# One vector through one partition and TensorE, and GpSimd's two kinds of values made together, in a four-layer graph attention kernel

## The reference

```python
h = jnp.einsum('nf,hfd->hnd', x, W)                 # 4 heads of 64
s_src = jnp.einsum('hnd,hd->hn', h, a[:, :64, 0])
s_dst = jnp.einsum('hnd,hd->hn', h, a[:, 64:, 0])
e = jax.nn.leaky_relu(s_src[:, :, None] + s_dst[:, None, :], 0.01)
e = jnp.where(adj[None, :, :] == 0, -jnp.inf, e)
out = jnp.einsum('hij,hjd->hid', jax.nn.softmax(e, axis=-1), h)
```

## Time and profile before

| | |
|---|---|
| median of 3 runs | 2998.18 us (2996.25 to 3000.05) |
| the profiled execution | 2995.74 us |
| its span, first to last instruction | 2993.9 us |
| TensorE busy | 2923.0 us, 98% |
| VectorE, ScalarE, GpSimd busy | 2133.9, 1920.6, 1179.6 us |
| mean granted clock of TensorE | 0.994 |

### The profile page before, as it was taken

How to read it: one execution, slowest core, us unless ns; L and a number is a source line. 1 busy time by engine, 2 the same in 40 slices (tenths; PEclk the granted TensorE clock), 3 DMA queues, 4 the chain that set the end, 5 groups by cost and what they waited for, 6 DMA issues and landing times.

```text
span 2993.9 us, 65253 instructions
## 1 busy us (share of the span) xinstructions
PE 2923.0 (98%) x24628; PEld 2556.9 (85%) x24628; DVE 2133.9 (71%) x3887; ACT 1920.6 (64%) x3414; POOL 1179.6 (39%) x1559
## 2 busy tenths in 40 slices
PE   7999999999989999999999999999999999989999
PEld 6899999999979999999998878887788878755555
DVE  5999898888888888888896556566666656562245
ACT  4777999999988999999985545444455444430000
POOL 0672385641226565654121023333323333444222
PEclk9999999999999999999999999999999999999999
DMA  8677100000100000000010000000000000000001
GB/s 292 207 234 246 39 11 15 11 11 14 62 15 13 11 15 11 15 11 15 11 35 12 4 1 4 4 1 4 1 4 4 1 1 1 3 1 1 0 14 42
DMA packets 41912, 104.55 MB, mean 35 GB/s; under 512 B 9856, under 2 KB 23424, under 8 KB 33536
## 3 DMA queue, kind: packets, MB, share of 16 engines
q1 hardware_dynamic: 39616, 101.61, 10.4%
q10 hardware_dynamic: 2112, 0.52, 0.1%
HBM read 97.73 MB, written 4.39 MB: 34 GB/s over the span
## 4 chain that ended last, share of the span: by engine, by line
PE 89%; DVE 5%; ACT 2%; issue 2%; DMA 1%; POOL 1%; SPq 0%; DVEq 0%; POOLq 0%; ACTq 0%
PE bank L1377 21%; PE bank L1380 21%; PE bank L1435 16%; PE bank L1473 13%; PE bank L1383 11%; PE bank L1308 2%; PE bank L1462 2%; DMA arena<-in_adj_dram 1%; PE bank L1449 1%; DVE rings L1804 1%; DVE arena L1724 1%; PE bank L1320 1%; ACT above L974 1%; PE bank L1358 1%; DVE rings L1799 1%
## 5 line engine op out<-in xcount | busy, mean ns | idle before, releaser
L1377 PE MATMUL bank<-values,rings 128*128 128x195 bf16 x8192 | 1392.1, 248 | 31.5 <-DVE rings L1807 19.0
L1380 PE MATMUL bank<-values,rings 128*128 128x195 bf16 x8192 | 1392.0, 248 | 0.0
L974 ACT ACTIVATE above<-srow,kpass 128x512 fp8e4<-128x512 f32 x2032 | 1279.9, 709 | 96.2 <-DVE rings L1807 87.1
L1377 PEld LDWEIGHTS bank<-values,rings 128*128 128x128 fp8e4 x8192 | 802.9, 98 | 44.0 <-issue 39.8
L1380 PEld LDWEIGHTS bank<-values,rings 128*128 128x128 fp8e4 x8192 | 802.9, 98 | 0.4
L1804 DVE TENSOR_TENSOR rings<-rings,above 128x512 uint32<-128x512 uint32 x512 | 387.1, 756 | 171.8 <-PE bank L1380 135.4
L1062 ACT ACTIVATE values<-srow,cmul 128x512 f32<-128x512 f32 x256 | 206.0, 815 | 411.5 <-PE bank L1473 410.5
L1807 DVE TENSOR_TENSOR rings<-rings 128x512 uint32<-128x512 uint32 x512 | 425.7, 831 | 17.3
L1473 PE MATMUL bank<-hv,values 128*128 128x257 f32 x1792 | 420.6, 380 | 0.0
L1473 PEld LDWEIGHTS bank<-hv,values 128*128 128x128 f32 x1792 | 335.0, 190 | 69.9 <-issue 25.2
L1383 PE MATMUL bank<-values,rings 128*128 128x390 bf16 x1920 | 318.7, 329 | 10.1 <-DVE values L1840 10.1
(11 more groups left out here) (223 smaller groups left out, 3483.5 us busy)
## 6 DMA issues: line engine op xcount, KB each, us to landing
arena<-in_adj_dram SPq DMA_DIRECT2D x64, 1024.0 KB, 4.9
srow<-src_dram SPq DMA_DIRECT2D x69, 256.0 KB, 3.1
x<-in_x_dram SPq DMA_DIRECT2D x4, 1024.0 KB, 11.4
out_dram<-x SPq DMA_DIRECT2D x7, 512.0 KB, 2.9
arena<-in_L_gnn_fe_w_dram SPq DMA_DIRECT2D x2, 512.0 KB, 7.2
arena<-in_L_gnn_W_hz_dram SPq DMA_DIRECT2D x1, 1024.0 KB, 7.7
arena<-in_L_gnn_g_w_dram SPq DMA_DIRECT2D x1, 1024.0 KB, 10.9
weights<-in_L_gnn_W_dram SPq DMA_DIRECT2D x3, 256.0 KB, 3.5
```

The costliest lines, as they stand in the source:

```text
L974: last = act.activation(above[:, k % 2, q, :], srow[:, par, :], ACT.Relu, scale=BIG, bias=kpass[:, p % 2, k * Q + q:k * Q + q + 1], satura ...
L1377: pe.matmul(acc[:, 0:KW], pos[:, k % 2, q, :].bitcast(FP8)[:, rows], v[:, 0:KW], start=start, stop=final, skip_group_check=True)
L1380: last = pe.matmul(acc[:, KP:KP + KW], neg[:, k % 2, q, :].bitcast(FP8)[:, rows], v[:, KP:KP + KW], start=False, stop=final, skip_group_ch ...
```

## The change

The attention vector of layer 0 is loaded in one transfer into partition 0 of `avec`, ahead of the weights on ScalarE's queue. TensorE multiplies a row of ones by it into bank 7, which leaves it on all 128 partitions, and VectorE reads it from there in the fold. GpSimd writes the row of ones and gives `s_const` before it makes `powers`, which get a semaphore of their own; TensorE waits for that one before the first packing. For layers 0 and 1 GpSimd makes both kinds in one row of instructions twice as wide (`both_kinds`), in the same two temporary buffers of 8 x 65 columns; layer 3 keeps the old function.

```diff
+        ones_row = sums[0:1, 0, :, :, :].rearrange("p t k c -> p (t k c)")[:, 0:P]
...
-        loaded_weights = [16 * 4, 16 * 13, 16 * 16, 16 * 18]
+        loaded_weights = [16 * 2, 16 * 11, 16 * 14, 16 * 16]
...
+        def both_kinds(eng, chain, l, j0, p, slot):
+
+            big, rest = (vtmp_pool[:, i].rearrange("p (k n) c -> p k n c", k=2) for i in range(2))
+            e = emul[:, :, p, ds(j0, GT)].unsqueeze(3)
+            rows = h[:, ds(j0, GT), p * D:(p + 1) * D].unsqueeze(1)
+            kinds = values[:, slot, ds(j0, GT), :].rearrange("p n (k w) -> p k n w", k=2)
+            part = [kinds[:, :, :, i * C:(i + 1) * C] for i in range(PARTS)]
+            eng.tensor_copy(big[:, :, :, D:C], e)
+            eng.tensor_tensor(big[:, :, :, 0:D], rows.to_broadcast([P, 2, GT, D]), e.to_broadcast([P, 2, GT, D]),
+                              ALU.mult).then_inc(chain.sem, 1)
+            eng.wait_ge(chain.sem, chain.next())
+            eng.nop(nofuse=True)
+            eng.tensor_copy(part[0], big).then_inc(chain.sem, 1)
...
+            eng.tensor_tensor(rest, big, part[0], ALU.subtract).then_inc(chain.sem, 1)
...
+            eng.tensor_copy(part[1], rest).then_inc(chain.sem, 1)
...
+            return eng.tensor_tensor(part[2], rest, part[1], ALU.subtract)
...
-            pool.memset(minus_half, -0.5).then_inc(s_pool, 1)
-            pool.wait_ge(s_pool, chain.next())
+            pool.memset(ones_row, 1.0)
+            pool.memset(minus_half, -0.5).then_inc(s_const, 1)
             for k in range(BITS):
                 last = pool.tensor_scalar(powers[:, k, :], ident[:, :], float(2 ** k), None, ALU.mult)
-            last.then_inc(s_const, 1)
+            last.then_inc(s_powers, 1)
+            pool.wait_ge(s_powers, 1)
...
-                for kind in range(2):
-                    made = value_parts(pool, chain, vtmp_pool, l, kind, g * GT, GT, p, p % 2)
+                if l < 3:
+                    made = both_kinds(pool, chain, l, g * GT, p, p % 2)
+                else:
+                    for kind in range(2):
+                        made = value_parts(pool, chain, vtmp_pool, l, kind, g * GT, GT, p, p % 2)
...
-                per_group = VALUE_LINKS * 2 + links
+                per_group = VALUE_LINKS * (1 if l < 3 else 2) + links
...
+            act.dma_start(avec[0:1, :, :].rearrange("p s (h d) -> p s h d", h=H),
+                          A["L0_gnn_a"].rearrange("h (s d) o -> o s h d", s=2)).then_inc(s_arow, 16)
             for k in range(2):
                 act.dma_start(weights[:, k, 0:F].rearrange("p (h d) -> p h d", h=H),
                               A["L0_gnn_W"][:, k * P:(k + 1) * P, :].rearrange("h p d -> p h d")).then_inc(s_w, 16)
-            for s in range(2):
-                act.dma_start(avec[:, s, :].rearrange("p (h d) -> p h d", h=H),
-                              A["L0_gnn_a"][:, s * D:(s + 1) * D, 0].partition_broadcast(P)).then_inc(s_w, 16)
...
             pe.wait_ge(s_const, 2)
+            pe.wait_ge(s_arow, 16)
+            pe.matmul(bank[7][:, 0:2 * F], ones_row, avec[0:1, :, :].rearrange("p s f -> p (s f)"),
+                      start=True, stop=True).then_inc(s_aps, 1)
...
+                            if q == 1:
+                                pe.wait_ge(s_powers, 1)
...
                 dve.wait_ge(s_w, loaded_weights[0])
+                dve.wait_ge(s_aps, 1)
...
-                                      avec[:, side:side + 1, :].to_broadcast([P, 2, F]), ALU.mult).then_inc(s_fold, 1)
+                                      bank[7][:, side * F:(side + 1) * F].unsqueeze(1).to_broadcast([P, 2, F]),
+                                      ALU.mult).then_inc(s_fold, 1)
```

More of the change, by code:

```diff
@@ L327, in gnn_kernel @@
         s_banksum = sem("bank_summed")
-        s_const = sem("constants_made")
+        s_const, s_powers = sem("constants_made"), sem("powers_made")
+        s_arow, s_aps = sem("attention_row_loaded"), sem("attention_row_in_psum")
         s_dve = sem("dve_chain")
```

## The result

The changed kernel takes **3048.36 us** (median of 4 runs, 3047.57 to 3050.12) beside 2998.61 us for the kernel before, measured with it: a ratio of 1.0168, with an interval of 1.015 to 1.0185. It is 50 us slower. The forecast of 3000.2 and its range of 2989 to 3010 are both missed; the sign of the forecast's sum was right and its size was wrong by more than 40 us.

What follows compares the result with a forecast made beforehand. TensorE, busy 2923.0 of 2993.9 us, was taken as the bound. Opening -1.1, front +1.9 and passes +1.2 gave +2.0 on the profiled 2995.74 (2997.7); the median, 2.4 above the profiled run, was forecast at 3000.2 us, range 2989 to 3010.

Steps and rivals of the forecast that it cites:

- The opening, -1.1 us: Before the first masks: 1016 fewer packets bring the adjacency's transfer and the masks 1.1 us earlier; ends 0 and -1.1.
- GpSimd's own time: Layers 0 and 1: merging saves GpSimd 1.7 us a pair, 80 us for 48 pairs, all beside TensorE.
- I take VectorE's total delay as unchanged: GpSimd's values: only instructions' data time shuts VectorE out, 3.6 us a pair either way, but pressed into fewer groups.
- There VectorE has just enough room: Passes behind the front, 350 to 400 us: TensorE is full although GpSimd is busy for 39.88 of 50 us.
- the passes at +1.2 us: Denser bursts at pass starts: 0.8 us in the first catch-up, 0.4 us at layer 1's opening; ends 0 and +8.
- The front, +1.9 us: 74 to about 340 us: the same delay in 0.6 groups less costs 1.9 us; ends -10.2 and +8.
- the longer instruction starves the masks: Rival, front and catch-up: VectorE's wait can grow from 0.45 to 0.9 us; +8 and +6, total 3011; chance 0.18.
- the catch-up: First pass behind the front: up to four pairs nearly in a row, 0.8 us; the rival priced the passes at +6.
- The rule for who is held: Front: the skill says the loser is blocked for the whole instruction; by it the term would be near -3, not +1.9.
- TensorE's waits for L1807 spread over all passes (then it is the length): Sign that the forecast is wrong: TensorE's waits for VectorE's masks in all passes would show that instruction length costs.

Runs made afterwards that it cites:

- e1: Kernel before with only the opening part of the change (vector on one partition, row of ones, signals), GpSimd's values as before; 2998.22 us, ratio 1.0001.
- e7: Kernel before, ScalarE's comparison of every fourth quarter in the looped passes cut to half its columns; 2998.01 us.
- e8: Kernel before with both kinds at once (old opening) and ScalarE's comparison of every fourth quarter in the looped passes cut to half its columns; 3049.89 us.
- e5: Kernel before with both kinds in one instruction but two tiles at a time, so as many instructions and elements each as before; 2998.57 us, ratio 1.0002.
- e3: Kernel before with only the copy and the two casts of the two kinds merged; 3008.23 us, ratio 1.0035.
- e13: Kernel before with both kinds at once (old opening) and 48 one-element GpSimd stores behind each self-wait of the chain; 3042.92 us, ratio 1.0151.
- e11: Kernel before with both kinds at once (old opening), VectorE's third mask operation cut to half its words in the looped passes; 3009.77 us, ratio 1.0039.
- e9: Kernel before with both kinds at once (old opening) and 16 one-element GpSimd stores behind each self-wait of the chain; 3019.82 us, ratio 1.0073.
- e2: Kernel before with only GpSimd's two kinds at once in layers 0 and 1, old opening; 3047.23 us, ratio 1.0164.
- e14: Kernel before with both kinds at once only for layer 0's second and third passes (16 of 48 groups), old opening; 3012.6 us, ratio 1.0049.
- e4: Kernel before, kinds apart, values of the looped passes of layers 0 and 1 made two tiles at a time (24 half-length instructions); 2994.35 us, ratio 0.999.

## Why the prediction was wrong, point by point

**The opening, -1.1 us: too small to tell from chance.** ScalarE's queue moved 1066 packets instead of 2112 and the first masks came at 61.51 instead of 63.19 (I had said 62.1). The timeline of the changed kernel's first 20 us:

```profile
6.04 2.04 PE L1690 MATMUL bank<-avec,sums 1*128 1x512 f32 x2 [6.04 <-DMA avec<-in_L_gnn_a_dram]
8.02 1.33 PE L1694 MATMUL bank<-ident 128*128 128x128 f32 x5
12.22 0.69 DVE L1746 TENSOR_TENSOR values<-weights,bank 128x512 f32<-128x512 f32 x1 [6.79 <-DMA weights<-in_L_gnn_W_dram]
14.99 3.51 PE L1336 MATMUL bank<-weights,values 128*128 128x264 f32 x8 [3.94 <-DVE weights L1750]
```

The fold starts at 12.22, not 9.7, and the dense products at 14.99, not 12.5. It waits for W, whose transfers I had placed by the old landing times of 5.7 and 8.1 us; behind the vector's row their median landing is 8.8 us, and the issue of the row ahead of them took 1.26 us where I had taken 0.6. The new product takes 2.04 us where I took 1.0 from the 128x264 row, and it delays the credit transposes from 6.58 to 8.02. None of it matters, as the step said: the masks follow the adjacency's transfer. e1 finds no gain of the whole opening, 1.0001. In the thirteen profiles with the old opening the first reduction starts anywhere from 66.36 to 69.21 (67.69 in e7, 69.21 in e8, the others in the table), in the four with the new one from 65.61 to 68.95, so 1.1 us at this place can't be told from chance. That variation should have been worth a sentence in the sum.

**GpSimd's own time: right in sign, half of what came.** I said some 70 to 80 us less; it is 137 us, which may be because a merged pair is also held by VectorE fewer times (that was not tested). It was worth nothing, as nothing waits for GpSimd in the passes.

**"I take VectorE's total delay as unchanged": the step that failed first.** The 512 instances of each of the three mask operations took 1073.4 us before (260.6 + 387.1 + 425.7) and 1125.2 us after:

```profile
L1839 DVE TENSOR_TENSOR rings<-rings,above 128x512 uint32<-128x512 uint32 x512 | 407.6, 796 | 174.5 <-PE bank L1408 132.9
...
L1842 DVE TENSOR_TENSOR rings<-rings 128x512 uint32<-128x512 uint32 x512 | 439.8, 859 | 17.3
...
L1834 DVE TENSOR_SCALAR rings<-packed 128x512 uint32 (+1 forms) x512 | 277.8, 543 | 1.3 <-ACT packed L974 1.2
```

The data time of GpSimd's instructions is the same, and the delay it causes is 52 us greater, 1.1 us a group. I had argued from data time alone, and no row excluded that a longer hold catches more of VectorE's time; the cost should have carried an upper end for it. That the form has no part in it is shown by e5, whose mask operations sum to 1075.9 us. Length is not all of it: in e3 they sum to 1104.4, though only the casts are longer there (0.82 us, where the unchanged products take 0.90) and what changed besides is that the products stand two and two. Nor does the total alone make the loss. In layer 1 the three operations take 530.4 us before, 559.2 after and 559.8 in e13, and the layer loses 26.3 us after and 11.5 us in e13. What counts besides the total is how much of it falls within a few units.

**"There VectorE has just enough room", the passes at +1.2 us: the step that carried the error.** I read the room from a window of 50 us: VectorE at 45.43 of 50 with TensorE full, so some 9% free and a burst can pass. But TensorE owns two buffers of masks, and VectorE may start on one only when TensorE has left it. So the free 9% can't be saved up. Over all units of the kernel before VectorE waits 171.8 us ahead of L1804, 0.34 us a unit of 2.7 us, of which some 0.2 us stand there in any case, and what a unit does not use is gone. Of the delay of 2.5 us above, within three units, 1.7 us were absorbed and 0.8 us reached TensorE. The 40 groups of values outside the front lose 44 us (17.8 in layer 0, 26.3 in layer 1) where the step had +1.2 and an upper end of 8. The view that shows it is the timeline of one unit with its bracket, [0.50 <-PE bank L1408], not the busy share. e11 and e9 test the two sides of this comparison, more room or less delay at a time, and each takes more than half of the loss away.

**The front, +1.9 us: too small, but inside its bounds.** The step spoke of the eight groups of head 1's values. Counted from the first reduction, the groups behind them are 6.8 us later than before in the changed kernel, 7.5 in e2 and 6.3 in e14; e1, with no merged values, is itself 1.7 later. The upper end was 8. What I had described can be seen: the delay is pressed into fewer groups, and part of it comes back. The first sums of the third group (before, then after) and of the fourth (after), where I had said 203 and the kernel before has 202.65:

```profile
173.40 0.55 DVE L1960 TENSOR_REDUCE sums<-bank 128x130 f32<-128x390 f32 x1
```

```profile
181.10 0.56 DVE L1995 TENSOR_REDUCE sums<-bank 128x130 f32<-128x390 f32 x1
...
207.90 0.56 DVE L1995 TENSOR_REDUCE sums<-bank 128x130 f32<-128x390 f32 x1
```

The third group is 7.7 us late and the fourth 5.25. Some of this may be TensorE's clock and not waits: at the granted clock of 0.95 from 150 to 200 us TensorE has 2.5 us less (an estimate, 0.05 of 50 us), which no run separates.

**The ends of the range.** For the passes the upper end was 0.2 us for each of 40 pairs, 8 us. Measured are 1.1 us for each of the 40, 44 us. The rival "the longer instruction starves the masks" names the right mechanism, a wait of VectorE that can grow from 0.45 to 0.9 us, and then prices it at +8 in the front, which is about what came there, and +6 in the passes, because I let it decide only "in the front and in the catch-up". Had its own number been carried through all 48 groups, two such waits in neighbouring units, 2 x 0.9 against room of 2 x 0.5, would have given 0.8 us a group, 38 us, by an estimate, and the range would have had to reach 3036. The sentence under "Against" (total data time is unchanged) is the failed step again: one assumption served both to make the forecast and to argue its rival down.

**The rule for who is held.** The Trainium skill, "SBUF — State Buffer", section "Who interferes with whom", says the loser of the shared access is blocked for the winner's whole instruction. By it I had worked out a better front (-3 instead of +1.9), as fewer fixed parts would be held. The front was 6 to 8 us slower, and e4 speaks against the fixed part too: with twice as many instructions in the loops VectorE's mask operations took 1063.2 us, and not more than the 1073.4 before. VectorE's 0.41 us operation of 563.05 was held for 0.95 us beside a product that ran from 562.74 to 564.13. That is until 564.00, all but the last 0.13 us of it; in rows 10 the hold also ends 0.12 us before the product does. So the trace agrees with the rule but for the instruction's last part; whether this is its fixed 0.17 us is not shown.

**What the list of signs said.** "TensorE's waits for L1807 spread over all passes (then it is the length)" is what came. The longest L1842 is 1572 ns, as I had said it would be if the instruction's length acted ("towards 1.6"). The line was right and cheap, and it tells why the forecast should have been less sure: I could name the sign and had no row against it.

## What to carry to other kernels

An instruction of GpSimd that runs beside a tightly buffered VectorE should be judged by how long it holds VectorE at once, and not by the engine time it saves: here six long instructions in place of twelve cost 1.07 us a group, and twenty-four short ones gained a little, where GpSimd had the time for them. The room of an engine between two buffers is read from the wait ahead of one unit in the timeline; a busy share of 91% over 50 us does not tell whether a delay of 1 us can be absorbed. And a gain for an engine that nothing waits for is worth nothing, however large (137 us here).

## What the runs showed that I had not expected

- The cost of merged instructions is not additive: 11 us (casts), 22 us (products), 49 us (both). 0.52 us of tiny stores between the long instructions takes 27 of the 49 back.
- A VectorE operation with a single input is held as well: L1834, 0.41 us alone, took 1.36 us beside GpSimd's 1.39 us product at 562.74.
- Sixteen stores of one element a partition take GpSimd 0.52 us, 33 ns each.
- With halves everywhere TensorE waits 40.5 us for GpSimd's values in layer 0 while layer 1 gains 3.5: GpSimd's number of instructions bounds the front, the length of each bounds VectorE in the passes.
